# Repeated masks for every weight chunk, another order on GpSimd and DVE, and a split last store

## The reference

```python
def _L0_cond_ref(x, y, weight, mask, bias):
    masked_w = weight * mask[None, :, :]
    w_bot = jnp.einsum('bg,got->bot', y, masked_w)
    return jnp.einsum('bnt,bot->bno', x, w_bot) + bias
x = x + _L0_cond_ref(x, cond_8, L0_cond_weight, L0_cond_mask, L0_cond_bias)
```

## Time and profile before

| what | value |
|---|---|
| three runs, median | 73.07 us |
| the profiled execution's own time | 72.25 us |
| its span, first to last instruction | 70.1 us |
| granted TensorE clock in it | 0.991 of full speed |
| first matmul of group 1 | 27.40 us |
| TensorE busy between 27.40 and 67.00 us | 39.44 of 39.60 us |
| transfers | 11.73 MB read, 8.39 MB written |

### The profile page before, as it was taken

One profiled execution on the slowest core, in us unless ns is written; L12 is line 12 of the kernel. 1 busy time (PEld: TensorE's weight loads), 2 busy tenths in 40 slices (PEclk: granted clock), 3 DMA queues, 4 the chain that ended last, 5 costly groups with the idle time before them and its releaser, 6 DMA issues.

```text
span 70.1 us, 1524 instructions
## 1 busy us (share of the span) xinstructions
PE 61.8 (88%) x666; PEld 57.7 (82%) x666; DVE 51.2 (73%) x34; ACT 45.0 (64%) x35; POOL 10.7 (15%) x16
## 2 busy tenths in 40 slices
PE   3997898847999973999999999999999999999910
PEld 3873786736988843999999999999999999999900
DVE  2207988938748999999993999999999199460040
ACT  3300476818579992049999999999922999504500
POOL 5400059980349000000000000000000000000000
PEclk9999999999999999999999999999999999999996
DMA  0999999999630003999899999999899721998383
GB/s 1 241 298 382 409 423 449 397 430 280 248 164 0 0 0 126 416 332 220 353 435 435 400 435 376 386 348 283 271 395 376 297 115 61 402 409 339 136 313 150
DMA packets 4901, 20.20 MB, mean 288 GB/s; under 512 B 544, under 2 KB 800, under 8 KB 3872
## 3 DMA queue, kind: packets, MB, share of 16 engines
q1 hardware_dynamic: 4752, 20.06, 76.3%
q10 hardware_dynamic: 144, 0.07, 0.4%
HBM read 11.73 MB, written 8.39 MB: 287 GB/s over the span
## 4 chain that ended last, share of the span: by engine, by line
PE 64%; DVE 18%; DMA 7%; issue 3%; SPq 2%; ACT 2%; ACTq 0%
PE slots L311 19%; PE slots L313 19%; PE slots L312 19%; DVE w_raw L452 7%; DMA weights<-in_weight 7%; PE slots L286 7%; DVE w_lo L436 5%; DVE x_lo L430 3%; DVE weights L423 2%; ACT w_hi L362 2%; SPq L157 1%; PE slots L277 1%; DVE weights L446 1%; SPq L154 1%; ACTq L380 0%
## 5 line engine op out<-in xcount | busy, mean ns | idle before, releaser
L311 PE MATMUL slots<-x_hi,w_hi 128*128 128x256 f32 x112 | 31.3, 280 | 1.6 <-DVE x_lo L430 1.6
L312 PE MATMUL slots<-x_lo,w_hi 128*128 128x256 f32 x112 | 31.3, 279 | 0.0
L313 PE MATMUL slots<-x_hi,w_lo 128*128 128x256 f32 x112 | 31.3, 279 | 0.0
L311 PEld LDWEIGHTS slots<-x_hi,w_hi 128*128 128x128 f32 x112 | 21.0, 188 | 1.9 <-issue 1.9
L312 PEld LDWEIGHTS slots<-x_lo,w_hi 128*128 128x128 f32 x112 | 21.0, 188 | 0.0
L313 PEld LDWEIGHTS slots<-x_hi,w_lo 128*128 128x128 f32 x112 | 21.0, 188 | 0.0
L436 DVE TENSOR_TENSOR w_lo<-w_raw,w_hi 128x2048 fp32r<-128x2048 f32 (+1 forms) x8 | 17.3, 2174 | 1.2 <-ACT w_hi L362 1.2
L430 DVE TENSOR_TENSOR x_lo<-x_ring,x_hi 128x2048 fp32r<-128x2048 f32 x7 | 16.0, 2286 | 2.9 <-ACT x_hi L356 2.7
L356 ACT CAST x_hi<-x_ring 128x2048 fp32r<-128x2048 f32 x6 | 11.4, 1906 | 6.5 <-DMA x_ring<-in_x 6.5
L371 ACT ACTIVATE weights<-slots,smalls 128x1024 f32<-128x1024 f32 x11 | 11.8, 1113 | 3.5 <-PE slots L313 3.5
L377 ACT COPY w_raw<-slots 128x1024 f32<-128x1024 f32 x8 | 8.0, 1013 | 9.3 <-PE slots L286 9.3
(11 more groups left out here) (21 smaller groups left out, 16.1 us busy)
## 6 DMA issues: line engine op xcount, KB each, us to landing
x_ring<-in_x SPq DMA_DIRECT2D x8, 1024.0 KB, 9.3
out<-weights SPq DMA_DIRECT2D x15, 512.0 KB, 6.0
weights<-in_weight SPq DMA_DIRECT2D x3, 512.0 KB, 6.4
x_ring<-in_mask SPq DMA_DIRECT2D x2, 512.0 KB, 6.4
weights<-in_weight SPq DMA_DIRECT2D x2, 256.0 KB, 3.9
out<-weights SPq DMA_DIRECT2D x2, 256.0 KB, 2.2
few_masks<-in_few SPq DMA_DIRECT2D x1, 128.0 KB, 2.4
smalls<-in_small ACTq DMA_DIRECT2D x1, 65.0 KB, 2.6
```

Of the source, the lines that this page charges most:

```text
L311: nc.tensor.matmul(dst, wh, xh, start=(k == 0), stop=False)
L312: nc.tensor.matmul(dst, wh, xl, start=False, stop=False)
L313: last = nc.tensor.matmul(dst, wl, xh, start=False, stop=(k == KC - 1))
```

## The change

- The masks of all four chunks are loaded repeated, 512 KB each, into the places of groups 1 and 2 of `x_ring` (`mask_of`). `few_masks`, the spreading on TensorE and its copy on DVE are gone. The mask of chunk 0 comes in two halves from ACT's queue with `smalls` between them. On SP the order is now weight, then mask. Group 1 of x is issued only when DVE has done its three products (`masked_by_dve`), since it lands where masks 0 and 1 were.
- DVE multiplies chunk 1 after its first copy of a unit, in place of its copy of unit 1; ACT makes both copies of unit 1. So `raw_act` and `raw_dve` count what each has done.
- GpSimd casts x of group 1 between its two gathers for h = 0 and its two for h = 1, instead of after all four. DVE subtracts x of group 1 ahead of the two halves of the weights, instead of behind them.
- In a unit the waits for masks stand behind the diagonal matmuls. Nine matmuls of zeros start TensorE, instead of five.
- The last half group is finished in three parts: 512 columns on ACT, 256 on DVE, and the last 256, which TensorE writes to a PSUM bank of their own, on ACT, which stores them from its own queue.

```diff
 RS = 3
 SLOTS = 4
-WARM = 5
+WARM = 9
...
-        masks = x_ring[:, XS - 1, :].rearrange("p (c f) -> p c f", c=CHUNKS - BY_SPREAD)
+        def mask_of(c):
+            return x_ring[:, 1 + c // 2, (c % 2) * SLOT:(c % 2 + 1) * SLOT]
...
+        def raw_act(u):
+            return u + 1 + (u >= 1)
+        def raw_dve(u):
+            return u + 1 - (u >= 1)
...
+        very_last = product(GROUPS - 2, 0)[:, 0:N]
...
-            sp.dma_start(few_masks[:], few).then_inc(few_loaded, 16)
             for h in range(2):
                 cols = slice(h * BANK, (h + 1) * BANK)
                 sp.dma_start(weights[:, 0, cols], weight[0, :, cols]).then_inc(first_loaded[h], 16)
-            sp.dma_start(weights[:, 1, :], weight[1]).then_inc(chunk_loaded[0], 16)
-            for c in range(BY_SPREAD, CHUNKS):
-                sp.dma_start(masks[:, c - BY_SPREAD, :], mask[c - BY_SPREAD]).then_inc(chunk_loaded[c - 1], 16)
+            for c in range(1, CHUNKS):
                 sp.dma_start(weights[:, c, :], weight[c]).then_inc(chunk_loaded[c - 1], 16)
-            for g in range(XS - 1):
-                load_group(g)
-            sp.wait_ge(masked_by_pool, CHUNKS - BY_SPREAD)
-            load_group(XS - 1)
+                sp.dma_start(mask_of(c), mask[c]).then_inc(chunk_loaded[c - 1], 16)
+            load_group(0)
+            sp.wait_ge(masked_by_dve, 3)
+            load_group(1)
+            sp.wait_ge(masked_by_pool, 2)
+            load_group(2)
...
-            for s, done in enumerate((out1_by_act, out1_by_dve)):
-                sp.wait_ge(done, GROUPS // 2 + s)
-                cols = slice(s * BANK, (s + 1) * BANK)
-                sp.dma_start(out[GROUPS - 1, 1, :, cols], result(GROUPS - 1, 1)[:, cols]
-                             ).then_inc(stored[SLOTS - 1], 16)
+            sp.wait_ge(last_by_act, 1)
+            sp.dma_start(out[GROUPS - 1, 1, :, 0:BANK], result(GROUPS - 1, 1)[:, 0:BANK]).then_inc(stored[SLOTS - 1], 16)
+            sp.wait_ge(last_by_dve, 1)
+            sp.dma_start(out[GROUPS - 1, 1, :, BANK:BANK + N], result(GROUPS - 1, 1)[:, BANK:BANK + N]
+                         ).then_inc(stored[SLOTS - 1], 16)
...
+            pool.wait_ge(chunk_loaded[1], 32)
+            nc.gpsimd.tensor_tensor(weights[:, 2, :], weights[:, 2, :], mask_of(2), ALU.mult).then_inc(masked_by_pool, 1)
+            pool.wait_ge(chunk_loaded[2], 32)
+            nc.gpsimd.tensor_tensor(weights[:, 3, :], weights[:, 3, :], mask_of(3), ALU.mult).then_inc(masked_by_pool, 1)
+            def gather(h, k):
+                unit = (h + 1) * CHUNKS - KC + k
+                pool.wait_ge(raw_by_act, raw_act(unit))
+                pool.wait_ge(raw_by_dve, raw_dve(unit))
+                at = k * RUNS // 2 + h * RUNS // 4
+                nc.gpsimd.tensor_copy(w_first(h, k).rearrange("p b (m r) -> p m b r", r=RT),
+                                      w_raw[:, at:at + RUNS // 4, 0:NB, :]).then_inc(w_first_ready, 1)
+            gather(0, 0)
+            gather(0, 1)
             pool.wait_ge(x_loaded[1], 16)
             nc.gpsimd.tensor_copy(x_hi[:, 1, :], x_ring[:, 1, :]).then_inc(x_hi_first, 1)
+            gather(1, 0)
+            gather(1, 1)
...
+                    pe.wait_ge(raw_by_act, raw_act(u - 2))
+                    pe.wait_ge(raw_by_dve, raw_dve(u - 2))
...
+                if u == 0:
+                    pe.wait_ge(smalls_loaded, 16)
+                if u == 2:
+                    pe.wait_ge(masked_by_dve, 3)
+                if c >= 2 and k == 0:
+                    pe.wait_ge(masked_by_pool, c - 1)
...
                         dst = product(g, h)[:, b * N:(b + 1) * N]
+                        if g == GROUPS - 1 and h == 1 and b == NB - 1:
+                            pe.wait_ge(out0_by_act, g)
+                            dst = very_last
...
-                        if g == GROUPS - 1 and h == 1 and b == 1:
-                            last.then_inc(last_half_ready, 1)
+                        if g == GROUPS - 1 and h == 1 and b in (1, 2):
+                            last.then_inc(last_ready, 1)
                     last.then_inc(products_ready, 1)
...
-            spread_masks()
             for u in range(UNITS):
                 weigh_unit(u)
...
+            act.dma_start(mask_of(0)[:, 0:BANK], mask[0, :, 0:BANK]).then_inc(first_loaded[0], 16)
             act.dma_start(smalls[:], small).then_inc(smalls_loaded, 16)
+            act.dma_start(mask_of(0)[:, BANK:SLOT], mask[0, :, BANK:SLOT]).then_inc(first_loaded[1], 16)
...
-            act.wait_ge(raw_by_dve, UNITS)
+                if u == 1:
+                    act.wait_ge(unit_ready, 2 * u + 2)
+                    nc.scalar.copy(raw_slot(u, 1), slots[:, 2 * (u % 2) + 1, :]).then_inc(raw_by_act, 1)
...
-            act.wait_ge(last_half_ready, 1)
+            act.wait_ge(last_ready, 1)
             act.wait_ge(stored[SLOTS - 1], 16 * (GROUPS // 2 - 1))
             nc.scalar.activation(result(GROUPS - 1, 1)[:, 0:BANK], product(GROUPS - 1, 1)[:, 0:BANK], ACT.Identity,
-                                 bias=bias(1)).then_inc(out1_by_act, 1)
+                                 bias=bias(1)).then_inc(last_by_act, 1)
+            act.wait_ge(products_ready, HO * GROUPS)
+            nc.scalar.activation(result(GROUPS - 1, 1)[:, SLOT - N:SLOT], very_last, ACT.Identity,
+                                 bias=bias(1)).then_inc(last_by_act, 1)
+            act.wait_ge(last_by_act, 2)
+            act.dma_start(out[GROUPS - 1, 1, :, SLOT - N:SLOT], result(GROUPS - 1, 1)[:, SLOT - N:SLOT]
+                          ).then_inc(stored[SLOTS - 1], 16)
...
-            dve.wait_ge(mask_spread, 1)
             for h in range(2):
-                dve.wait_ge(first_loaded[h], 16)
-                cols = weights[:, 0, h * BANK:(h + 1) * BANK].rearrange("p (q t) -> p q t", t=T)
-                nc.vector.tensor_tensor(cols, cols, few_wide[:, 2 * h:2 * h + 2, 0, :], ALU.mult).then_inc(masked_by_dve, 1)
-            dve.wait_ge(chunk_loaded[0], 16)
-            cols = weights[:, 1, :].rearrange("p (q t) -> p q t", t=T)
-            nc.vector.tensor_tensor(cols, cols, few_wide[:, :, 1, :], ALU.mult).then_inc(masked_by_dve, 1)
+                dve.wait_ge(first_loaded[h], 32)
+                cols = slice(h * BANK, (h + 1) * BANK)
+                nc.vector.tensor_tensor(weights[:, 0, cols], weights[:, 0, cols], mask_of(0)[:, cols],
+                                        ALU.mult).then_inc(masked_by_dve, 1)
...
             for u in range(UNITS):
-                dve.wait_ge(unit_ready, 2 * u + 2)
-                nc.vector.tensor_copy(raw_slot(u, 1), slots[:, 2 * (u % 2) + 1, :]).then_inc(raw_by_dve, 1)
+                if u == 1:
+                    dve.wait_ge(chunk_loaded[0], 32)
+                    nc.vector.tensor_tensor(weights[:, 1, :], weights[:, 1, :], mask_of(1), ALU.mult).then_inc(masked_by_dve, 1)
+                else:
+                    dve.wait_ge(unit_ready, 2 * u + 2)
+                    nc.vector.tensor_copy(raw_slot(u, 1), slots[:, 2 * (u % 2) + 1, :]).then_inc(raw_by_dve, 1)
+            low_x(1)
             low_weights(1, 0, 2)
             low_weights(1, 2, 4)
-            low_x(1)
...
-            finish(GROUPS - 1, slice(BANK, SLOT))
+            dve.wait_ge(last_ready, 2)
+            dve.wait_ge(stored[SLOTS - 1], 16 * (GROUPS // 2 - 1))
+            nc.vector.tensor_scalar(result(GROUPS - 1, 1)[:, BANK:BANK + N], product(GROUPS - 1, 1)[:, BANK:BANK + N], bias(1),
+                                    None, ALU.add).then_inc(last_by_dve, 1)
```

More of the change, by code:

```diff
@@ L34, with conditional_residual @@
 SLOTS = 4
-WARM = 5
+WARM = 9
 AT_BIAS = B * RT
 SMALL = AT_BIAS + HO
-def conditional_residual(nc, x, small, weight, few, mask, out):
-    assert QU * T == SLOT == 2 * BANK and O == N == T and QU * B * RT == BANK and R * BY_SPREAD == ROWS
-    assert SPAN * 2 == P and QU * RT * 2 == ROWS and KC == HO == BY_SPREAD == 2 and TILES == QU == NB == SLOTS
+def conditional_residual(nc, x, small, weight, mask, out):
+    assert QU * T == SLOT == 2 * BANK and O == N == T and QU * B * RT == BANK
+    assert SPAN * 2 == P and QU * RT * 2 == ROWS and KC == HO == 2 and TILES == QU == NB == SLOTS
     with ExitStack() as ctx:
@@ L437, in low_weights, with finish @@
                                         ALU.subtract).then_inc(w_lo_ready, 1)
[L439 removed]
+            def finish(g):
                 j = 2 * g + 1
@@ L492 @@
     arrays, args = {}, []
-    for name, a in (("x", x_in), ("small", small), ("weight", weight_in), ("few", few), ("mask", mask_in)):
+    for name, a in (("x", x_in), ("small", small), ("weight", weight_in), ("mask", mask_in)):
         a = np.ascontiguousarray(a)
```

69 lines of the change are left out of this document (15 added, 54 removed).

## The result

Four runs of the changed kernel gave 74.41, 74.57, 74.84 and 75.46 us, median **74.7 us**; the kernel before had 73.62 in the same comparison. The ratio was 1.0256, 95% interval [1.0155, 1.0357]. Twelve more runs of the same changed kernel (the last experiment) give 74.64 us and the firmer ratio **1.0158 [1.0102, 1.0213]**, so the change costs about 1.2 us. I had forecast 73.4 and no measurable change. Ratios here compare only executions within 1.5% of the quickest one of the same kernel, so where many executions lie outside I tell the median of all as well.

What follows compares the result with a forecast made beforehand. Bound by when group 1 can start (loads, GpSimd and DVE ahead of it), then gapless TensorE and the end: 72.25 + 0.75 - 0.4 = 72.6 us profiled, 73.07 + 0.35 = 73.4 us median; range 72.0 to 74.8.

Steps and rivals of the forecast that it cites:

- the choice in the part on GpSimd: Before group 1: both h = 1 gathers run ahead of DVE's low x, so DVE starts at 23.25, group 1 at 28.15.
- The rival that DVE gets in between the two gathers: Group 0, h = 1: DVE's subtraction delays the second gather to 25.5; group 0 +1.8 us, kernel 74.5 us; chance 0.22.
- the 0.34 us of issue ahead of group 1: Between DVE's last low weights, done at 27.8, and TensorE's start of group 1 at 28.15: 0.34 us of issue.
- The loads: Start of kernel: 896 KB more on full DMA engines costs 2.24 us; x of group 1 lands at 20.3.
- The pause of unit 5: TensorE's earlier 0.88 us pause in unit 5, taken as late code, would not return: cost 0.
- The second half of mask 0: Chunk 0's loads: the second half would land at 6.7, with 384 KB more ahead of it.
- a term at nothing: TensorE in unit 0: it ends at about 8.0 as before, so dropping the spreading is worth nothing.
- The slack in the middle: Group 2's low weights stay 0.36 us ahead of TensorE's need, so the 39.6 us of gapless matmuls hold.
- The end: Last half group: ACT's 256 columns gain 0.27 us, the smaller store 0.13; -0.4 us, between -0.6 and -0.1.
- 0.65 us for the units: Units before group 0: all 0.65 to 0.7 us late, so group 0 can start at 19.35.
- 2.2 for x: Loads of x for groups 0 and 1: each lands 2.2 us later, at 17.9 and 20.3.

Runs made afterwards that it cites:

- e1: Changed kernel with both halves of chunk 0's mask issued on SP's queue instead of ACT's: 75.38 us, ratio 1.0291.
- e2: Changed kernel with nine more matmuls of zeros in TensorE's pause inside unit 0, to hold the clock: 74.09 us, ratio 1.0144.
- e9: Changed kernel with DVE's product of chunk 1 ahead of its copy of unit 0: 74.75 us, ratio 1.012.
- e12: Changed kernel run again unedited, beside the kernel before: 74.64 us, ratio 1.0158.
- e6: Changed kernel with DVE's low part of x waiting for all four gathers: 74.41 us, ratio 1.002.
- e10: Changed kernel with nine more zero matmuls, DVE's chunk 1 product before its unit 0 copy, and low x waiting for all four gathers: 72.83 us, ratio 0.996.
- e8: Changed kernel with low x waiting for all four gathers and nine more zero matmuls in unit 0's pause: 73.48 us, ratio 0.9981.
- e7: Kernel before with only the new three-part finish of the last half group: 72.51 us, ratio 0.9937.
- e4: Changed kernel with the old order of group 1 on GpSimd (four gathers, then cast) and DVE (weights, then x): 74.58 us, ratio 1.0129.
- e11: Kernel before, spread masks kept, with the new order, low x waiting for all four gathers, and the new end: 72.31 us, ratio 0.967.

## Why the prediction was wrong

**The step that failed** is the choice in the part on GpSimd: "so I let both gathers go first". Only the first did. The rival that DVE gets in between the two gathers, to which I gave 0.22, is what happened, in every profile of the new order without the wait: I had the second gather end at 25.5, group 0 at 29.2 and the kernel at 74.5; it was 25.83, 29.59 and 74.64 us. The reason I gave (GpSimd has them queued, DVE has to hear of the cast) was true and did not help. In e1 and e2 DVE had been idle and did wait for the cast, and its subtraction came 0.08 and 0.09 us behind the start of the first gather; in e9 and e12 it came 0.09 and 0.14 us behind it. There it stood waiting for 0.3 to 0.4 us (it took 2.62 to 2.67 us instead of 2.28) and then went ahead of the second gather, although the copies that this gather needs were done by then:

```profile
22.82 2.62 DVE L431 TENSOR_TENSOR x_lo<-x_ring,x_hi 128x2048 fp32r<-128x2048 f32 x1
```

That is e12's row, to be read beside its gathers at 22.68 above. In the profile of the result the two things fall together: the second gather also needs DVE's copy of the last unit, which ended at 23.13, and the subtraction stands right behind that copy and began at 23.04. My forecast had that copy done at 20.75.

In e6 and e10 both gathers do go first. From the start of the cast to group 1 the forecast had 7.8 us, and these two have 7.76 and 7.75. (Two small terms of that sum were off and cancelled: I started DVE at 23.25, before the 23.4 of my own second gather, and the 0.34 us of issue ahead of group 1 was 0.19 us of waiting in e6.) e6's group 1 at 27.96 is close to the forecast's 28.15, and its ratio of 1.002 [0.9961, 1.0079] to the 1.0045 of 73.4 against 73.07. With the 1.2 us between e2 and e8 this shows the choice at the gathers as the step that failed. The Trainium skill (SBUF — State Buffer, Who interferes with whom) says that a DVE instruction with two SBUF inputs contends with a GpSimd instruction that reads SBUF, and that of two contenders the first to issue holds the pair for its whole instruction; the trace agrees (3.23 for 1.17, 2.54 for 0.61), if issue is counted per instruction. I had stretched it to a run of two.

**The rest of the error**, from a forecast of 72.6 for the profiled execution to 74.84: group 1 came 1.44 later than forecast (1.04 between cast and group 1, 0.4 by x landing later), the middle cost 0.83, the end 0.2, and 0.2 less lay outside the span.

- *The loads* were right where they mattered. Mask 1 landed at 9.3 (9.2), chunk 2 at 11.94 (11.7), chunk 3 at 14.4 (14.3), x at 18.2 and 20.7 (17.9 and 20.3). The pause of unit 5, which I costed at 0, did not return. The second half of mask 0 was wrong, 8.58 instead of 6.7. It cost TensorE 2.5 us of pause, and it held up the copy of unit 0 and with it the product of chunk 1 behind that copy, which then collided with GpSimd's (3.28 instead of 2.36). Group 0 started 2.4 us after the forecast (21.77 for 19.35). By the table only the late issue of x reached group 1, with the 0.5 us that e9 wins back; the rest was covered by the wait for the gather. That cover is luck: with both gathers first, as forecast, group 0 would have ended at 21.77 + 7.17 = 28.94, 0.8 us after the forecast start of group 1. So a term at nothing, the pause in unit 0 and the clock after it, was wrong as well, hidden by the larger error.
- *The slack in the middle* did not hold. Before, the 1.55 us of idle time ahead of group 1 was what gave DVE its time to finish group 0 and split group 2. Now group 1 starts the moment group 0 ends, DVE's finish, low x and low weights take 29.71 to 35.39, and TensorE wants them at 29.59 + 5.6 = 35.2. The next, x of group 3, is only issued at the end of group 0 and landed at 34.8, with ACT idle 5.03 us before it. So groups 1 and 2 took 5.90 and 5.89 us from start to start instead of 5.60, 0.3 each; in e6, where group 1 waits for DVE again, 5.71 and 5.73. The other 0.25 is five later groups at 5.65 to 5.69 instead of 5.60; in e12 the last three had 5.60, so not every execution of the changed kernel has it, and its cause stays open. I had taken a difference of two times that move together, and one of them moved alone.
- *The end* was right in kind, -0.22 in the profile and -0.45 by e7, against -0.4, both between my bounds of -0.6 and -0.1. ACT took 0.47 for 256 columns (0.48 forecast), the smaller store gained nothing that the profile shows.
- *The repeated masks cost time.* e4 and e7 both have the old order and the new end. They differ in the masks and in what came with them (the place of DVE's product of chunk 1, ACT's second copy, four more matmuls of zeros, the waits in a unit; of these only the place of the product was tried, in e9): 1.0129 [0.9988, 1.027] and 0.9937 [0.9888, 0.9986], 1.9% or about 1.4 us, uncertain by about 1 us by the two intervals. e10 and e11, with the new order and the wait, point the same way (72.83 and 72.31 us by all runs). These costs were in my sum at 0.65 us for the units and 2.2 for x; what was left of them there had been set off against the new order's gain.

So the change is a trade: by these runs the masks lose about 1.4 us, the end gains 0.45, and the new order shows no gain without the wait: under repeated masks old order, new order, and new order with the wait gave 1.0129, 1.0158 and 1.002. Only the last two are told apart.

## What to carry to other kernels

Two instructions in a row on GpSimd are two chances for DVE to take the shared port: if a third engine waits for the second one, make DVE's two-input operation wait for it too, and read the length of short GpSimd instructions first when a start is late. A cost that a longer wait covers, as the half clock here, comes back when that wait is repaired, so measure it again then. Bytes put ahead of a transfer that ends a chain cost about their full time on full DMA engines (896 KB, 2.24 us by the rate: x landed 2.6 us later, 2.1 in e9), and an earlier issue wins little of it back (2.6 us sooner issued, 0.5 sooner landed). A slack between two engines holds only while both start from the same event; before counting on one, ask whether the idle time that makes it is the very thing the change removes.

## What the runs showed of the hardware

- GpSimd's place between two gathers is not kept for it: a DVE subtraction that had come 0.08 to 0.14 us after the first gather's start went ahead of the second in four profiles (e1, e2, e9, e12), and the second gather took 2.67 us instead of 0.61.
- Of a DVE product with two SBUF inputs and a GpSimd product the later one waits: GpSimd's took 3.28 instead of 2.36 us when DVE's had begun 0.15 us sooner, DVE's took 3.29 instead of 1.22 when GpSimd's had begun 0.13 us sooner. So a tenth of a microsecond decides which one pays. DVE paid in the two longest executions profiled (e4's 77.92 us, e8's 76.67); that this widens the spread of the runs is likely, not shown.
- TensorE's granted clock fell to 0.50, the 1.2 GHz level, and stood there from 9 to 15 us in one execution of the changed kernel, after a pause of 2.49 us, and did not fall in another, after 2.19. The length of the pause doesn't decide it alone: in e6 the clock stood at 0.50 from 9 to 12 us after a pause of 2.03, in e7, with spread masks, after one of 1.14.
- A half mask of 256 KB issued at 1.66 on ACT's queue landed at 8.58, after a chunk of 512 KB issued at 1.65 on SP's (7.95). In the first 12 us ACT's queue moved 0.59 MB in 432 packets, 1.4 KB each, SP's 3.15 MB in 1001, 3.1 KB each. The Trainium skill (DMA: Bandwidth & Descriptors, Queues, rings and completion order) says that an engine takes turns between its queues packet by packet; with packets of such sizes ACT's queue would get the smaller share, which would fit. That was not tested by itself: in e1, with everything on SP's queue, the half landed near 7.9, in an execution whose chunk 2 came 1.1 us later than in the changed kernel's profile.
